# Delta-rule attention slots on one Trainium2 core: two groups of transposes and one copy change places

## The chip, the core and the metric

The kernel runs on one core of a Trainium2 chip. The core has five engines, each with an in-order instruction queue: Tensor (matrix products and transposes into PSUM; the profile calls it PE, and its weight loads PEld), Vector (DVE), Scalar (ACT), GpSimd (POOL) and Sync (SP), which here only issues DMAs. The engines wait for each other through semaphores. The metric is the time on the device in microseconds (us), lower is better. The granted clock of Tensor is given as a share of its full speed, 2.4 GHz.

## What is computed

The reference is a two-layer model on an input of 4 x 512 tokens of width 256. Each layer adds an attention and a feed-forward branch to its input:

```python
x  = L0_attn_x                                # 4 x 512 x 256
xn = _layernorm(x)
x  = x + _L0_attn_ref(xn, ...) + _L0_ffn_ref(xn, ...)
xn = _layernorm(x)
x  = x + _L1_attn_ref(xn, ...) + _L1_ffn_ref(xn, ...)

# attention, in both layers: 16 key heads, 32 value heads of 128
mixed = silu(causal_conv_of_4_taps(xn @ W_qkv))     # -> q, k, v
q = l2norm(q) * 128 ** -0.5;  k = l2norm(k)
def step(S, (q, k, v, g, beta)):                    # one token
    S = S * exp(g)
    u = (v - k @ S) * beta
    S = S + outer(k, u)
    return S, q @ S
# then a root-mean-square norm, a gate silu(z) and @ W_out
```

The change touches the attention only. The feed-forward branches are a mixture of six experts (layer 0) and a table-coded network (layer 1).

## The kernel before

**Tiling.** The recurrence over tokens is replaced by its chunked form. A sequence is cut into 4 chunks of 128 tokens (`CHUNKS`), the four sequences are worked on side by side (`BATCH`), and each key head (`KHEADS`, 16) serves a group of two value heads (`GROUPS`). One pass of the function `body` over (key head h, chunk c) is a slot; a layer has 64 of them, in the order of `steps`, and the file has one `body` for each engine, whose statements are that engine's queue. Within a slot an engine does the attention of slot (h, c) and, mixed into it, the preparation of the next one, (nh, ncn): the projections of q, v and z, the convolution, the transposes of keys and queries, their squares for the norms, and the decays.

**A slot on Tensor** (all in `body` of `block.tensor`). `fill(t)` is a projection of six matrix products (L837), t = 0 to 4. Between the five of them lie the steps of the inverse of a 128 x 128 triangular matrix, which is put together from its blocks: L896 (first group, its result is copied by Scalar at L1098), L909 (second group, read by Vector at L1292), L921 and L926 (turned blocks and the third group, which wait for Vector's L1292), and L939 (the last corner, which waits for Scalar's copies of Z, L1103, and of X, L1115). The last term of projection 2 stands behind the wait for L1292. The next slot's keys are transposed by `keys_token_major` (L849, four transposes) ahead of L909, the queries by `queries_token_major` (L859) behind the wait for Z and ahead of L939. Then follow, in chunks 1 to 3, the products with the state (L950, which waits for the corner copies L1124, and L957), the key products L866, then L969, L977 (not in chunk 3), L981, the values' transposes L877 (which wait for Vector's L1259), the outputs' transposes L996 and the output projection L1005. In layer 1 the gate is taken first (`gate_first`): L996 waits for Vector's L1279. In layer 0 L996 waits for Scalar's L1168, and L1005 for L1279.

**A slot on Scalar.** Its queue is: scaled keys of group 0 (L1093), the first convolution input (`copy_mix`, L1030 and L1031), the copy of Z's first part (L1098), scaled keys of group 1, then `square_keys` (the copy L1068 of the transposed keys and four squares L1059), `copy_mix` of 1, the queries' silu (L1051), `copy_mix` of 2, `copy_right` (L1115), two `copy_z` (L1103), `copy_left` (L1119), in chunk 2 three weight splits (L1040), silu of z (L1045), `square_queries` (four squares, L1059), `copy_corner` (L1124), silu of z and of the values, and later the copies for the second half of the slot. In chunk 3 there are no scaled keys.

**A slot on Vector.** Convolution of q (three L1204, which start when Scalar's L1031 of that tile is done), L1292 on the second group's result, convolution of value head 0, `key_columns` (L1212 to L1218), convolution of value head 1, in chunk 2 weight splits (L1344), `query_columns` (L1224, which waits for the queries' squares), the diagonals (L1232), in chunks 1 to 3 L1309 on the product L950, the decay scans (L1243), L1252, L1255, L1259, the state's update (L1265 or L1271), the gates (L1279) and the residual (L1337).

**Order.** It is written out by hand in the three bodies. Sync loads rows, keys, products and inverse blocks for the next slots; GpSimd computes the scaled queries and two powers. Neither is touched by the change.

Of the kernel before, what the change touches and what calls it, by code (L numbers as in the profile page):

```python
# [623 lines left out]
def delta_attention(nc, m, L, d):  # L624

    gate_first = L == 1
    with ExitStack() as ctx:
# [103 lines left out]
        def pj_bank(c, t):  # L731

            return pj[:, (c + t) % 2, :]

        def following(h, c):
            return (h, c + 1) if c + 1 < CHUNKS else (h + 1, 0)

        with nc.Block() as block:
# [83 lines left out]
            def _(pe):  # L822
                def project(h, c, t, k, first, terms=(0, 1, 2)):


                    q = 4 * h + c
                    if k == 0 and terms[0] == 0:
                        if c == 0:
                            pe.wait_ge(w_high_ok, PROJS * h + t + 1)
                            pe.wait_ge(w_low_ok, PROJS * h + t + 1)  # L830
                        if t >= 2 or not first:
                            pe.wait_ge(pj_read, PROJS * q + t - 1)
                    at = slice(HALO + c * P, HALO + (c + 1) * P)
                    pairs = ((w_high, m.x_high), (w_high, m.x_low), (w_low, m.x_high))
                    for n in terms:
                        wt, xt = pairs[n]
                        ins = nc.tensor.matmul(pj_bank(c, t), wt[:, k, t, :], xt[:, k, :, at],  # L837
                                               start=(k == 0 and n == 0), stop=(k == KD - 1 and n == 2))
                    if k == KD - 1 and terms[-1] == 2:
                        ins.then_inc(proj_mm, 1)  # L840

                def keys_token_major(h, c, first):

                    q = 4 * h + c
                    pe.wait_ge(k_in[c % 2], 16 * (2 * h + c // 2 + 1))
                    if not first:
                        pe.wait_ge(vn_ok, 2 * q - 1)
                    for b in range(BATCH):
                        ins = nc.tensor.transpose(kk[:, 0, bank(b)], kq[:, c % 2, b, 0, :], eye)  # L849
                    ins.then_inc(ktok_mm, 1)  # L850

                def queries_token_major(h, c, first):

                    q = 4 * h + c
                    pe.wait_ge(q_silu, q + 1)
                    if not first:
                        pe.wait_ge(vn_ok, 2 * q)
                    for b in range(BATCH):
                        ins = nc.tensor.transpose(kk[:, 1, bank(b)], kq[:, c % 2, b, 1, :], eye)  # L859
                    ins.then_inc(qtok_mm, 1)  # L860
# [19 lines left out]
                def body(h, c, first, last):  # L880
                    it = 4 * h + c
                    nh, ncn = following(h, c)

                    def fill(t):
                        if not last:
                            project(nh, ncn, t, 0, False)
                            project(nh, ncn, t, 1, False)
# [11 lines left out]
                    fill(1)  # L899
                    pe.wait_ge(xd_in, 64 * (it + 1))  # L900
                    pe.wait_ge(z32_cp, it + 1)
                    if not last:
                        keys_token_major(nh, ncn, False)
                    if not first:
                        for g in range(GROUPS):
                            pe.wait_ge(res_ok[g], BATCH * it)
# [3 lines left out]
                                                   Z[half(g), 0, part(b)], start=True, stop=True)  # L910
                    ins.then_inc(dx_mm, 1)
                    if not last:
                        project(nh, ncn, 2, 0, False)
                        project(nh, ncn, 2, 1, False, (0, 1))
                    pe.wait_ge(w_blocks_in, 64 * (it + 1))
# [8 lines left out]
                    for b in range(BATCH):  # L924
                        for g in range(GROUPS):
                            ins = nc.tensor.matmul(gb[HALF:, 0, g, part(b)], corner_a[half(g), c % 2, b, :],  # L926
                                                   W[half(g), b, 0:HALF], start=True, stop=True)
                            if b == BATCH - 1:
                                ins.then_inc(z64_mm[g], 1)
                    fill(3)  # L930
                    pe.wait_ge(x_in, 32 * (it + 1))
                    pe.wait_ge(x_cp, 4 * it + 1)
                    for g in range(GROUPS):
                        pe.wait_ge(z_cp[g], it + 1)
                    if not last:
                        queries_token_major(nh, ncn, False)
                    for b in range(BATCH):
                        for g in range(GROUPS):
                            ins = nc.tensor.matmul(gb[half(g), 0, g, part(b)], Z[HALF:, g, part(b)],  # L939
# [80 lines left out]
            def _(act):  # L1020
# [21 lines left out]
                def silu_z(h, c, g):  # L1042
                    q = 4 * h + c
                    act.wait_ge(proj_mm, PROJS * q + CONVS + g + 1)
                    nc.scalar.activation(zT[:, c % 2, g, :], pj_bank(c, CONVS + g), ACT.Silu).then_inc(pj_read, 1)  # L1045
# [9 lines left out]
                def square(w):  # L1055

                    for b in range(BATCH):
                        n = w * BATCH + b
                        ins = nc.scalar.activation(sq_kq[:, bank(n)], kk[:, w, bank(b)], ACT.Square,  # L1059
                                                   accum_out=ss_kq[:, n:n + 1])  # L1060
                    return ins
# [9 lines left out]
                def square_queries(h, c):  # L1071
                    q = 4 * h + c
                    act.wait_ge(qtok_mm, q + 1)
                    square(1).then_inc(q_sq, 1)
# [21 lines left out]
                def copy_z32(it):  # L1096
                    act.wait_ge(z32_mm, it + 1)
                    nc.scalar.activation(Z[:, 0, 0:BATCH * HALF], gb[:, 1, 0, 0:BATCH * HALF],  # L1098
                                         ACT.Copy).then_inc(z32_cp, 1)
# [18 lines left out]
                def copy_left(it):  # L1118
                    nc.scalar.activation(corner(X, low, low), turned(1, low, HALF), ACT.Copy).then_inc(x_cp, 1)  # L1119

                def copy_corner(it):
                    for g in range(GROUPS):
                        act.wait_ge(x64_mm[g], it + 1)
                        nc.scalar.activation(by4(X[low, g, :])[:, :, high],  # L1124
                                             gb[half(g), 0, g, 0:BATCH * HALF].rearrange("p (b n) -> p b n", b=BATCH),
                                             ACT.Copy, scale=-1.0).then_inc(x_cp, 1)

                def body(h, c, first, last):
                    it = 4 * h + c
                    nh, ncn = following(h, c)  # L1130
                    if c < CHUNKS - 1:
                        scaled_keys(h, c, 0)
                    if not last:
                        copy_mix(nh, ncn, 0, False)
                    copy_z32(it)
                    if c < CHUNKS - 1:
                        scaled_keys(h, c, 1)
                    if not last:
                        square_keys(nh, ncn, False)
                        copy_mix(nh, ncn, 1, False)  # L1140
                        silu_conv(nh, ncn, 0)
                        copy_mix(nh, ncn, 2, False)
                    copy_right(it)
                    for g in range(GROUPS):
                        copy_z(g, it)
                    copy_left(it)
                    if c == 2 and h < KHEADS - 1:
                        for t in range(CONVS):
                            split_weights(h + 1, t)
                    if not last:  # L1150
                        silu_z(nh, ncn, 0)
                        square_queries(nh, ncn)
                    copy_corner(it)
                    if not last:
                        silu_z(nh, ncn, 1)
                        for t in range(1, CONVS):
                            silu_conv(nh, ncn, t)
                    if c == 2 and h < KHEADS - 1:
                        for t in range(CONVS, PROJS):
                            split_weights(h + 1, t)  # L1160
                    for g in range(GROUPS):
                        act.wait_ge(y_mm[g], it + 1)
                        nc.scalar.activation(y[:, g, :], gb[:, 0, g, :], ACT.Copy,  # L1163
                                             scale=-1.0 if c else 1.0).then_inc(y_cp[g], 1)
                    if not gate_first:
                        for g in range(GROUPS):
                            act.wait_ge(o_mm[g], it + 1)
                            nc.scalar.activation(oT[:, g, :], gb[:, 1, g, :], ACT.Copy).then_inc(o_cp[g], 1)  # L1168
                    for g in range(GROUPS):
                        act.wait_ge(sso_mm[g], it + 1)  # L1170
                        for b in range(BATCH):
                            ins = nc.scalar.activation(Z[:, g, bank(b)], gb[:, 0, g, bank(b)], ACT.Square,  # L1172
                                                       accum_out=ss_o[:, g, b:b + 1])
                        ins.then_inc(o_sq[g], 1)
                    if not last:
                        scaled_values(nh, ncn)
# [639 lines left out]
```

## Time and profile before

| | us |
|---|---|
| median of 3 runs | 4951.69 (4949.87 to 4952.98) |
| the profiled execution's own time | 4951.72 |
| its span, first to last instruction | 4949.9 |
| Tensor busy | 4443.0 (90%) |
| Vector busy | 3852.1 (78%) |
| Scalar busy | 2999.4 (61%) |
| GpSimd busy | 692.1 (14%) |

The profiled execution agrees with the median, so times read in its trace can be set against either. The first slot of layer 0 begins at about 782 us and the last of layer 1 at about 4917 us; between the layers lie the feed-forward branches, the norm and the preparation of the inverse blocks. Slots of the same chunk look alike through a layer, so a slot can be read once for each chunk.

How to read a trace row: start in us from the start of the span, duration, engine, line of the kernel, operation, the tile written and the tiles read, their shapes, and how many instructions are merged in the row. Brackets give the idle time of the engine just before, and the instruction that ended it by its semaphore; "issue" is an idle time for which the profile names none. Tensor's instructions are pipelined, and their ends are modelled.

### The profile page before, as it was taken

To read this page: it belongs to the slowest core of one execution; us is meant where nothing else is said; L and a number is where in the kernel's file an instruction comes from. 1 tells how busy PE (TensorE), PEld (TensorE's weight loads), DVE (VectorE), ACT (ScalarE), POOL (GpSimd) and SP (SyncE) were. 2 spreads that over 40 slices of the span, in tenths; PEclk is the share of its full clock that TensorE was granted. 3 is DMA by queue.
4 is the path that set the end of the run, shared out by engine and by line. 5 is a ranking of instruction groups with operands and counts; after the bars stand their busy time and mean duration, and the time that the engine had idled before them with its cause. 6 is when DMAs were issued, how large, how long until landed. Compare 5 with 4: busy or idle time off the path is not lost. (4 is left out here: it accounts for less than half of the span.)

```text
span 4949.9 us, 93402 instructions
## 1 busy us (share of the span) xinstructions
PE 4443.0 (90%) x32596; PEld 3643.5 (74%) x32596; DVE 3852.1 (78%) x8126; ACT 2999.4 (61%) x9834; POOL 692.1 (14%) x740
## 2 busy tenths in 40 slices
PE   5899937999999999999969988299999999999998
PEld 3577736888888888888845877188888888887887
DVE  6838887888888888888841587788888888888886
ACT  1145526777777777777611555366666676767665
POOL 0000001122121221212200000021212122221211
PEclk8999968999999999999969999599999999999999
DMA  1035543222232222222200555322222222222222
GB/s 56 28 96 158 166 123 92 77 82 75 79 87 72 80 71 85 80 77 80 61 30 15 144 165 166 100 77 77 83 73 79 72 81 74 80 76 80 71 80 63
DMA packets 637757, 422.56 MB, mean 85 GB/s; under 512 B 458344, under 2 KB 533656, under 8 KB 636846
## 3 DMA queue, kind: packets, MB, share of 16 engines
q1 hardware_dynamic: 637294, 416.62, 29.2%
q8 instruction: 262, 4.29, 0.4%
q14 instruction: 201, 1.65, 0.1%
HBM read 296.24 MB, written 120.16 MB: 84 GB/s over the span
## 5 line engine op out<-in xcount | busy, mean ns | idle before, releaser
L1204 DVE SCALAR_TENSOR_TENSOR conv_l<-mix_l,taps_l,conv_l 128x512 f32<-128x512 f32 x1152 | 865.0, 751 | 270.3 <-ACT conv_l L1031 243.0
L837 PE MATMUL pj_l<-x_high,w_high_l 128*128 128x512 f32 x1280 | 588.2, 460 | 160.3 <-ACT w_high_l L1040 160.3
L837 PE MATMUL pj_l<-x_high,w_low_l 128*128 128x512 f32 x1280 | 521.1, 407 | 41.8 <-DVE W_l L1292 41.8
L837 PE MATMUL pj_l<-x_low,w_high_l 128*128 128x512 f32 x1280 | 512.5, 400 | 0.0
L1406 POOL TENSOR_TENSOR fac_l<-den_l,powers 128x4 f32<-128x4 f32 x256 | 258.0, 1008 | 1783.7 <-DVE den_l L1327 1779.8
L1005 PE MATMUL gb_l<-wo_l,gT_l 128*128 128x256 f32 x2048 | 478.7, 384 | 0.0
L1172 ACT ACTIVATE Z_l<-gb_l 128x128 f32<-128x128 f32 x1024 | 267.9, 289 | 307.1 <-PE gb_l L996 307.1
L1005 PEld LDWEIGHTS gb_l<-wo_l,gT_l 128*128 128x128 f32 x2048 | 372.6, 190 | 67.8 <-ACT Z_l L1172 24.4
L1337 DVE SCALAR_TENSOR_TENSOR x<-gb_l,fac_l,x 128x256 f32<-128x256 f32 x1024 | 413.0, 477 | 9.0
L837 PEld LDWEIGHTS pj_l<-x_high,w_high_l 128*128 128x128 f32 x1280 | 241.6, 189 | 231.3 <-ACT w_high_l L1040 160.9
L1163 ACT ACTIVATE y_l<-gb_l 128x512 f32<-128x512 f32 x256 | 153.2, 598 | 397.8 <-PE gb_l L969 393.1
L837 PEld LDWEIGHTS pj_l<-x_high,w_low_l 128*128 128x128 f32 x1280 | 241.6, 189 | 148.4 <-issue 93.3
L1243 DVE TENSOR_TENSOR_SCAN decay_l<-rows_l,diag_b_l 128x512 f32<-128x512 f32 x256 | 300.3, 1215 | 0.0
L1082 ACT ACTIVATE vn_l<-kk_l,ncol_l 128x128 f32<-128x128 f32 x1024 | 284.7, 438 | 17.2 <-PE kk_l L877 17.2
L1030 ACT ACTIVATE mix_l<-pj_l 128x512 f32<-128x512 f32 x384 | 238.8, 622 | 69.3 <-PE pj_l L837 58.9
L1031 ACT ACTIVATE conv_l<-pj_l,taps_l 128x512 f32<-128x512 f32 x384 | 274.6, 715 | 0.0
L1379 POOL TENSOR_TENSOR ncol_l<-n_l,powers 128x4 f32<-128x4 f32 x128 | 130.3, 1018 | 1013.2 <-DVE n_l L1212 1013.2
L837 PEld LDWEIGHTS pj_l<-x_low,w_high_l 128*128 128x128 f32 x1280 | 242.9, 190 | 35.2
L1059 ACT ACTIVATE diag_b_l<-kk_l 128x128 f32<-128x128 f32 x1024 | 268.0, 280 | 0.1
L981 PE MATMUL gb_l<-ap_l,y_l 128*128 128x128 f32 x2048 | 267.2, 276 | 0.0
L620 DVE TENSOR_TENSOR lane_t_l<-lane_t_l,lane_step_l 128x336 f32<-128x336 f32 (+16 forms) x540 | 252.1, 467 | 18.6
L617 DVE TENSOR_TENSOR lane_step_l<-lane_k_l,lane_t_l 128x336 f32<-128x336 f32 (+16 forms) x540 | 251.2, 465 | 18.6
(203 smaller groups left out, 10449.0 us busy)
## 6 DMA issues: line engine op xcount, KB each, us to landing
rows_l<-rows_dram SPq DMA_DIRECT2D x128, 1024.0 KB, 5.5
k_dram<-kT_l SPq DMA_DIRECT2D x128, 256.0 KB, 2.3
kk_dram<-key_kkS_l SPq DMA_DIRECT2D x128, 256.0 KB, 2.4
kq_l<-k_dram SPq DMA_DIRECT2D x128, 256.0 KB, 3.2
kkS_l<-kk_dram SPq DMA_DIRECT2D x128, 256.0 KB, 5.7
w_raw_l<-in_wx SPq DMA_DIRECT2D x32, 640.0 KB
own_dram<-key_kkS_l SPq DMA_DIRECT2D x1024, 16.0 KB, 1.7
lane_k_l<-own_dram SPq DMA_DIRECT2D x32, 512.0 KB, 4.4
```

Of the source, the lines that this page charges most:

```text
L620: nc.vector.tensor_tensor(t[:, :, j + 1:, 0:j], t[:, :, j + 1:, 0:j], prod, ALU.subtract).then_inc(solve, 1)
L837: ins = nc.tensor.matmul(pj_bank(c, t), wt[:, k, t, :], xt[:, k, :, at], start=(k == 0 and n == 0), stop=(k == KD - 1 and n == 2))
L981: ins = nc.tensor.matmul(gb[:, 1, g, bank(b)], y[:, g, bank(b)], ap[:, c % 2, g, b, 1, :], start=(c == 0), stop=True, skip_group_check=True)
L1005: ins = nc.tensor.matmul(gb[:, b // 2, g, (b % 2) * DIM:(b % 2 + 1) * DIM], gT[:, g, bank(b)], wo[:, g, :], start=True, stop=True)
L1031: nc.scalar.activation(conv[:, t, :], pj_bank(c, t), ACT.Copy, scale=taps[:, h, t, HALO:HALO + 1]).then_inc(pj_read, 1)
L1059: ins = nc.scalar.activation(sq_kq[:, bank(n)], kk[:, w, bank(b)], ACT.Square, accum_out=ss_kq[:, n:n + 1])
L1082: ins = nc.scalar.activation(vn[:, g, bank(b)], kk[:, g, bank(b)], ACT.Copy, scale=ncol[:, b:b + 1])
L1172: ins = nc.scalar.activation(Z[:, g, bank(b)], gb[:, 0, g, bank(b)], ACT.Square, accum_out=ss_o[:, g, b:b + 1])
L1204: ins = nc.vector.scalar_tensor_tensor(out, mix[:, t, :, i:i + P], wt(i), out, ALU.mult, ALU.add)
L1243: nc.vector.tensor_tensor_scan(decay[:, g, :], rows[:, c % 2, g, 0, :], diag_b[:, g, :], 0.0, ALU.mult, ALU.add).then_inc(decay_ok, 1)
L1337: nc.vector.scalar_tensor_tensor(xt, gb[:, b // 2, g, (b % 2) * DIM:(b % 2 + 1) * DIM], fac[:, g, b:b + 1], xt, ALU.mult, ALU.add).then_in ...
L1406: nc.gpsimd.tensor_tensor(fac[:, g, :], den[:, g, :], m.powers[:, 1, :], ALU.pow).then_inc(fac_ok[g], 1)
```

## The change

Three pieces of the hand-written order change; no instruction is added, removed or altered. On Tensor, `keys_token_major` of the next slot stands behind L909 instead of ahead of it, and `queries_token_major` stands ahead of the waits for the X and Z copies instead of behind them; the waits inside these two functions move with them. On Scalar, `copy_corner` stands ahead of `square_queries` in chunks 1 to 3, and stays behind it in chunk 0.

```diff
@@ -899,8 +899,6 @@
                     fill(1)
                     pe.wait_ge(xd_in, 64 * (it + 1))
                     pe.wait_ge(z32_cp, it + 1)
-                    if not last:
-                        keys_token_major(nh, ncn, False)
                     if not first:
                         for g in range(GROUPS):
                             pe.wait_ge(res_ok[g], BATCH * it)
@@ -910,6 +908,7 @@
                                                    Z[half(g), 0, part(b)], start=True, stop=True)
                     ins.then_inc(dx_mm, 1)
                     if not last:
+                        keys_token_major(nh, ncn, False)
                         project(nh, ncn, 2, 0, False)
                         project(nh, ncn, 2, 1, False, (0, 1))
                     pe.wait_ge(w_blocks_in, 64 * (it + 1))
@@ -928,12 +927,12 @@
                             if b == BATCH - 1:
                                 ins.then_inc(z64_mm[g], 1)
                     fill(3)
+                    if not last:
+                        queries_token_major(nh, ncn, False)
                     pe.wait_ge(x_in, 32 * (it + 1))
                     pe.wait_ge(x_cp, 4 * it + 1)
                     for g in range(GROUPS):
                         pe.wait_ge(z_cp[g], it + 1)
-                    if not last:
-                        queries_token_major(nh, ncn, False)
                     for b in range(BATCH):
                         for g in range(GROUPS):
                             ins = nc.tensor.matmul(gb[half(g), 0, g, part(b)], Z[HALF:, g, part(b)],
@@ -1149,8 +1148,12 @@
                             split_weights(h + 1, t)
                     if not last:
                         silu_z(nh, ncn, 0)
+                    if c > 0:
+                        copy_corner(it)
+                    if not last:
                         square_queries(nh, ncn)
-                    copy_corner(it)
+                    if c == 0:
+                        copy_corner(it)
                     if not last:
                         silu_z(nh, ncn, 1)
                         for t in range(1, CONVS):
```

## Rows read from the trace of the kernel before

**Rows 1.** Busy time by stage, layer 1: stretch, length, engines, granted clock, DMA.

```profile
3300.00:4900.00 1600.00, 1534.84 (x12831) 1295.36 (x12831) 1325.70 (x2981) 1100.11 (x4020) 317.68 (x339) 1.00 0.27 77
```

**Rows 2.** Timeline of Scalar, layer 1, chunk 1; the last row from chunk 2.

```profile
4103.53 0.60 ACT L1068 ACTIVATE ktok_l<-kk_l 128x512 f32<-128x512 f32 x1
...
4108.12 0.63 ACT L1103 ACTIVATE Z_l<-gb_l 64x256 f32<-64x256 f32 x2
...
4109.78 0.28 ACT L1059 ACTIVATE diag_b_l<-kk_l 128x128 f32<-128x128 f32 x1
...
4110.70 0.22 ACT L1059 ACTIVATION_READ_ACCUMULATOR diag_b_l<-kk_l 128x1 f32 x1
4110.80 0.79 ACT L1124 ACTIVATE X_l<-gb_l 64x256 f32<-64x256 f32 x2
...
4138.78 0.26 ACT L1059 ACTIVATE diag_b_l<-kk_l 128x128 f32<-128x128 f32 x1
```

**Rows 3.** Timeline of Tensor, layer 1, chunk 1, first part of the slot.

```profile
4102.86 0.60 PE L849 MATMUL kk_l<-eye,kq_l 128*128 128x128 f32 x4
4103.39 0.68 PE L909 MATMUL gb_l<-Z_l,Xd_l 64*64 64x64 f32 x16
...
4105.78 0.47 PE L837 MATMUL pj_l<-x_high,w_low_l 128*128 128x512 f32 x1 [0.33 <-DVE W_l L1292]
...
4108.47 0.39 PE L837 MATMUL pj_l<-x_high,w_low_l 128*128 128x512 f32 x1
4109.11 0.63 PE L859 MATMUL kk_l<-eye,kq_l 128*128 128x128 f32 x4 [0.26 <-issue]
4109.67 0.68 PE L939 MATMUL gb_l<-X_l,Z_l 64*64 64x64 f32 x16
```

**Rows 4.** Timeline of Vector, layer 1, chunk 1; the last two rows from chunk 2.

```profile
4102.03 2.33 DVE L1204 SCALAR_TENSOR_TENSOR conv_l<-mix_l,taps_l,conv_l 128x512 f32<-128x512 f32 x3 [1.51 <-ACT conv_l L1031]
4104.39 1.24 DVE L1292 TENSOR_SCALAR W_l<-gb_l 32x128 f32<-32x128 f32 x4
4106.26 2.33 DVE L1204 SCALAR_TENSOR_TENSOR conv_l<-mix_l,taps_l,conv_l 128x512 f32<-128x512 f32 x3 [0.63 <-ACT conv_l L1031]
...
4111.23 0.16 DVE L1224 TENSOR_SCALAR qcol_l<-ss_kq_l 128x4 f32<-128x4 f32 x1
...
4112.90 2.16 DVE L1309 SCALAR_TENSOR_TENSOR vn_l<-gb_l,run_columns_l,vn_l 128x128 f32<-128x128 f32 x8 [0.30 <-PE gb_l L950]
...
4140.34 0.17 DVE L1224 TENSOR_SCALAR qcol_l<-ss_kq_l 128x4 f32<-128x4 f32 x1
...
4141.82 0.87 DVE L1309 SCALAR_TENSOR_TENSOR vn_l<-gb_l,run_columns_l,vn_l 128x128 f32<-128x128 f32 x3
```

**Rows 5.** Timeline of Tensor at the ends of four slots, layer 1, chunks 0 to 3.

```profile
4095.26 0.66 PE L996 MATMUL gb_l<-eye,gT_l 128*128 128x128 f32 x4 [0.46 <-DVE gT_l L1279]
...
4123.37 0.66 PE L996 MATMUL gb_l<-eye,gT_l 128*128 128x128 f32 x4 [0.20 <-DVE gT_l L1279]
...
4152.96 0.65 PE L996 MATMUL gb_l<-eye,gT_l 128*128 128x128 f32 x4 [0.88 <-DVE gT_l L1279]
...
4177.76 0.86 PEld L877 LDWEIGHTS kk_l<-eye,vT_l 128*128 128x128 f32 x8 [0.23 <-DVE ap_l L1259]
```

**Rows 6.** Timeline of Vector's gates and Tensor's output projections, layer 0, chunks 0 to 2.

```profile
1658.16 1.28 DVE L1279 TENSOR_TENSOR gT_l<-zT_l,gb_l 128x512 f32<-128x512 f32 x2
1659.31 3.82 PE L1005 MATMUL gb_l<-wo_l,gT_l 128*128 128x256 f32 x16
...
1685.79 1.28 DVE L1279 TENSOR_TENSOR gT_l<-zT_l,gb_l 128x512 f32<-128x512 f32 x2
1687.19 3.82 PE L1005 MATMUL gb_l<-wo_l,gT_l 128*128 128x256 f32 x16
...
1715.15 1.28 DVE L1279 TENSOR_TENSOR gT_l<-zT_l,gb_l 128x512 f32<-128x512 f32 x2
1715.89 3.81 PE L1005 MATMUL gb_l<-wo_l,gT_l 128*128 128x256 f32 x16
```

## What the change will do to the time

> **What bounds the kernel now.** I read four views. First the table of stages: over 1600 us of the second layer's attention Tensor is busy 1535 us, Vector 1326, Scalar 1100, at a granted clock of 1.00 [rows 1]. By shares this is Tensor's stage. Then, because the change only reorders work inside a slot, I read one slot in order of time on each engine, and looked for where an engine stands still and who ends it. A slot is one of the 64 steps (key head, chunk) of a layer; I write its times as the trace has them, for chunk 1 of one head.
>
> Scalar [rows 2]: from the copy of the transposed keys (L1068, 4103.53) to the end of the corner copies (L1124, 4111.59) it runs without one idle mark. It is an in-order queue: keys' copy and squares, the convolution inputs, the copies of Z, silu, queries' squares, corner. The keys' transposes end on Tensor at 4102.86 + 0.60 = 4103.46 [rows 3], and the keys' copy starts 0.07 later. So that whole stretch of eight us hangs on the keys' transposes, in chunk 1.
>
> Vector [rows 4]: the second convolution starts at 4106.26 after 0.63 idle, ended by Scalar's L1031, in that stretch. From there to L1224 at 4111.23 nothing stops it; then comes 0.30 idle before L1309, ended by Tensor's L950, and after that it is loaded to the end of the slot. In chunk 2 the same place has no idle mark.
>
> The end of the slot [rows 5]: in layer 1 the second half of Tensor's L996 waits for Vector's gate L1279: 0.46 us in chunk 0, 0.20 in chunk 1, 0.88 in chunk 2. In chunk 3 it is L877 at 4177.76 whose weights load waits 0.23 for Vector's L1259. So in all four slots of a layer 1 head Tensor ends its slot behind Vector, and Vector behind Scalar, and Scalar behind the keys' transposes. The holes Tensor has earlier in the slot are not what sets the period. In layer 0, L1005 waits for the first gate: the gate pair starts at 1658.16, 1685.79 and 1715.15, one gate takes about 0.68 (half of a pair's 1.28 and an overlap of 0.08), so it is ready at 1658.84, 1686.47 and 1715.83; L1005 starts at 1659.31, 1687.19 and 1715.89 [rows 6]. With 0.06 for the handover, Vector is 0.41, 0.66 and 0 us ahead in chunks 0, 1 and 2.
>
> **The change, part by part.** No instruction is added or removed, no DMA is moved; waits travel with their groups.
>
> *Keys' transposes behind L909.* Before, they take Tensor at 4102.86 and L909 follows at 4103.39. After, L909 stands first. It lasts 0.68 with some 0.07 of overlap, so the transposes start about 0.61 later and, since a group of 64-wide tiles does not start as tightly behind a projection as they do, up to 0.69 later; lower bound 0.60, I take s = 0.65, the middle. Who gains: L909's reader on Vector is L1292, which starts at 4104.39, right behind the convolution that began at 4102.03 and lasts 2.33 [rows 4]: end 4104.36. An earlier L909 (it ended at 4104.07) gives at most 0.03. So the hole of 0.33 before the last projection term, ended by L1292 [rows 3], stays: Tensor has the same work ahead of that wait in either order. Who loses: Scalar. Queued behind the keys' copy are both convolution inputs, the Z copies and silu, and Vector's second convolution waits for one of them. All move by s: Z's second copy ends at 4108.12 + 0.63 + 0.65 = 4109.40.
>
> *Queries' transposes ahead of the wait for Z.* They now start at 4109.11, and the projection before them would have let them start at 4108.71 (its terms follow each other every 0.24, the last from 4108.47). This 0.40 us hole, put down to issue, is filled. L939 then has to wait for Z's copies itself. The transposes start 0.36 after the copies' end (4109.11 against 4108.12 + 0.63 = 4108.75) [rows 2, 3], with six conditions to pass; L939 will have four, so I give it 0.27 to 0.36: it starts at 4109.67 to 4109.76. It starts at 4109.67 today. The gain of this edit, 0.40, is eaten by s exactly. It costs nothing: the queries' silu stands ahead of the Z copies in Scalar's queue, so it is done when they are needed at 4108.71.
>
> *Corner ahead of squares, chunks 1 to 3.* The squares start at 4109.78 today, right behind the silu [rows 2]. The corner takes their place: 4109.78 + 0.65 = 4110.43. The corner copies run from 4110.43 to 4111.22 (L939 ends at 4109.67 + 0.68 = 4110.35, in time); the squares start 0.75 behind their start, the overlap taken off, and last 1.14 (4109.78 to 4110.70 + 0.22), to 4112.32. Today they end at 4110.92 and Vector takes L1224 at 4111.23, not waiting. After the change Vector would be there at 4111.88 and stands until 4112.36, 0.04 being the handover. L1224 to L1309 takes 1.48 in chunk 2 where no idle is marked [rows 4], of which 0.12 is a gap that I can't assign, so 1.36 to 1.48: L1309 starts at 4113.72 to 4113.84, not 4112.90. That is 0.82 to 0.94 later; I take 0.88. What the earlier corner buys is L950, and Tensor waits for Vector at L996 anyway. In chunk 2 both queues hold weight splits ahead of this place: the squares start at 4138.78 today, so they will end at 4138.78 + 0.65 + 0.75 + 1.14 = 4141.32, and L1224 comes at 4141.36 instead of 4140.34, 1.02 later; no idle behind it takes any of that. Chunk 3 is like chunk 1. Chunk 0 keeps its order: Vector moves by 0.65, and has no L1309 whose idle could absorb any.
>
> **The sum.** Layer 1: each slot's end moves with Vector: 0.65 + 0.88 + 1.02 + 0.88 = 3.43 us a head. Layer 0: chunk 0 has 0.41 of lead, so 0.24; chunk 1 0.88 - 0.66 = 0.22; chunk 2 1.02; chunk 3 0.88, since I take its tie at L877 to be that of layer 1: 2.36. Sixteen heads: 54.9 + 37.8 = 92.7. The last slot of each layer has no next one (1.8 less) and the last head's chunk 2 has no weight split, as chunk 1 (0.9 less): 90 us. The profiled execution took 4951.72 us (span 4949.9), the median of the runs is 4951.69, so both give 5042 us, 1.8% slower. With the low ends (s 0.60, 1.36) the same sum gives 79 us, with the high ends (0.69, 1.48) 99 us: 5031 to 5050.
>
> The Trainium skill, page "Perfetto Trace Analysis", section "Identifying the Most-Contended Engine", says to take the engine with the highest occupancy as the bottleneck, though it warns that matmul busy time misleads for Tensor. By that, closing Tensor's holes gains, which is rival A; the waits at L996 and L877 disagree with it here.
>
> **Rivals.**
> A. *Tensor is the bound* and the filled holes count; ends faster. The place is L859: 0.40 us in 126 slots, 50 us. For: Tensor is busy 96% [rows 1]. Against: Z's copies are Scalar's, and Scalar follows the keys' transposes. It decides from an s under about 0.05. As layer 1 waits at L996 all the same, only layer 0's 63 slots can bring it: 25 us, 4927 us; in both layers 50 us, 4902 us.
> B. *Only the keys' delay counts*: the squares come in time though they stand behind the corner (Scalar catching up by 0.5 us). Then L1309 in chunks 1 and 3 moves by 4111.88 + 1.42 - 4112.90 = 0.40, chunks 0 and 2 by 0.65: 2.10 a head in layer 1, and 0.24 + 0 + 0.65 + 0.40 = 1.29 in layer 0: 54 us less 1, 5005 us. For: Scalar is busy only 1100 of 1600 us [rows 1]. Against: its idle time does not lie between the keys' copy and the corner.
> C. *Nothing moves*: the filled hole and the delay cancel at L939, as worked out, and the way over Vector has slack that I don't see. Then 4952 us. For: layer 0's leads in chunks 0 and 1. Against: the marks at L996 and the tie at L877.
> D. *The clock falls too.* The granted clock is 1.00 over the stage though chunk 2 has a hole of 0.88 [rows 1, 5]; this hole would grow to 1.9 us. If Tensor came out of each on the lower level (1.2 GHz), L1005's pass of 3.82 us [rows 6] would take up to twice that in 32 slots: 122 us more, 5164 us.
> "TensorE: Matmul & The Clock Gate" of the Trainium skill, section "What's actually happening", says that idling throttles the array's clock; no run here shows it for holes of this size.
>
> **How the numbers follow.** The likeliest is the sum as worked out, chance 0.65: 5042. B has 0.14, times between the two included; A 0.10; C 0.06; D 0.05. The range goes from just under B to above the sum's high end: 5003 to 5058; it leaves out A, C and D, 0.21, about 2 in 10. A measurement of this kernel can tell some 0.2% (10 us) from no change. Faster by more: 0.10. Within: 0.06. Slower by more: 0.84.
>
> **What would show it.** In the changed profile: keys' copy on Scalar 0.60 to 0.69 later in the slot, with an idle mark ended by the transposes in every chunk; no issue hole at the queries' transposes, and a new one before L939, which starts at the same time in the slot as today; Vector's idle before the second convolution 1.2 to 1.3 instead of 0.63; a new idle of about 0.5 before L1224, ended by Scalar's squares, in chunks 1 to 3; L996's holes in layer 1 near 1.1, 1.1 and 1.9. The sum is wrong if L1292 starts earlier with L909, if Scalar's stretch shows idle marks that swallow s, or if L996 and L877 no longer wait for Vector.

## The result and the profile after

The changed kernel takes 5044.42 us (median of 4, 5042.76 to 5048.51) against 4951.65 us before: the ratio is 1.0187, with a 95% interval of 1.0172 to 1.0202. It is slower by 1.9%; the profiled execution took 5042.76 us, with a span of 5041.0. All engines execute the same numbers of instructions. The profile's table of busy times, with the share of the span in parentheses:

```profile
PE 4451.6 (88%) x32596; PEld 3647.0 (72%) x32596; DVE 3855.5 (76%) x8126; ACT 2992.0 (59%) x9834; POOL 691.6 (14%) x740
```

The busy table of the stretch of [rows 1] after the change has the granted clock still at 1.00, and Tensor at 1490 of 1600 us instead of 1535:

```profile
3300.00:4900.00 1600.00, 1490.03 (x12384) 1252.58 (x12384) 1286.49 (x2895) 1058.94 (x3876) 307.55 (x328) 1.00 0.26 74
```

The slot of chunk 1 that answers to [rows 2 to 4] starts at 4164.27 (its L896; before, 4100.72). Most line numbers are shifted: L907 is the old L909, L938 the old L939, L949 the old L950, L995 the old L996, L1067 the old L1068, L1102 the old L1103, L1123 the old L1124, L1207 the old L1204, L1227 the old L1224, L1312 the old L1309, L1262 the old L1259, L1282 the old L1279. Timeline of Tensor:

```profile
4164.27 0.69 PE L896 MATMUL gb_l<-Te_l,ap_l 128*64 128x64 f32 x16
...
4166.49 0.68 PE L907 MATMUL gb_l<-Z_l,Xd_l 64*64 64x64 f32 x16
4167.11 0.66 PE L849 MATMUL kk_l<-eye,kq_l 128*128 128x128 f32 x4
4169.34 0.47 PE L837 MATMUL pj_l<-x_high,w_low_l 128*128 128x512 f32 x1 [0.39 <-DVE W_l L1295]
...
4172.26 0.60 PE L859 MATMUL kk_l<-eye,kq_l 128*128 128x128 f32 x4
4173.16 0.68 PE L938 MATMUL gb_l<-X_l,Z_l 64*64 64x64 f32 x16 [0.30 <-ACT Z_l L1102]
```

Timeline of Scalar, same slot:

```profile
4167.80 0.60 ACT L1067 ACTIVATE ktok_l<-kk_l 128x512 f32<-128x512 f32 x1 [0.81 <-PE kk_l L849]
...
4172.39 0.63 ACT L1102 ACTIVATE Z_l<-gb_l 64x256 f32<-64x256 f32 x2
...
4174.02 0.78 ACT L1123 ACTIVATE X_l<-gb_l 64x256 f32<-64x256 f32 x2
4174.82 0.28 ACT L1058 ACTIVATE diag_b_l<-kk_l 128x128 f32<-128x128 f32 x1
...
4175.75 0.22 ACT L1058 ACTIVATION_READ_ACCUMULATOR diag_b_l<-kk_l 128x1 f32 x1
```

Timeline of Vector, same slot:

```profile
4167.95 1.24 DVE L1295 TENSOR_SCALAR W_l<-gb_l 32x128 f32<-32x128 f32 x4
4170.53 2.33 DVE L1207 SCALAR_TENSOR_TENSOR conv_l<-mix_l,taps_l,conv_l 128x512 f32<-128x512 f32 x3 [1.34 <-ACT conv_l L1030]
...
4176.00 0.17 DVE L1227 TENSOR_SCALAR qcol_l<-ss_kq_l 128x4 f32<-128x4 f32 x1 [0.41 <-ACT diag_b_l L1058]
4177.40 0.87 DVE L1312 SCALAR_TENSOR_TENSOR vn_l<-gb_l,run_columns_l,vn_l 128x128 f32<-128x128 f32 x3
```

The times below are differences to the slot's start. The keys' copy on Scalar stood at 4103.53 - 4100.72 = 2.81 and stands at 3.53, behind 0.81 of idle ended by the keys' transposes. The second convolution on Vector stood at 5.54 and stands at 6.26; its idle time grew from 0.63 to 1.34. Tensor's L938 stood at 8.95 and stands at 8.89: the queries' transposes have filled the hole ahead of it (L859 has no bracket now), and a wait for Z (0.30) has taken its place. L1227 stood at 10.51 and stands at 11.73, and L1312 stood at 12.18 and stands at 13.13.

The ends of slots that answer to [rows 5], layer 1, chunks 0 to 3 (timeline of Tensor; the last row is a weights load):

```profile
4158.82 0.66 PE L995 MATMUL gb_l<-eye,gT_l 128*128 128x128 f32 x4 [0.54 <-DVE gT_l L1282]
...
4187.87 0.66 PE L995 MATMUL gb_l<-eye,gT_l 128*128 128x128 f32 x4 [0.97 <-DVE gT_l L1282]
...
4215.25 1.09 PE L877 MATMUL kk_l<-eye,vT_l 128*128 128x128 f32 x8 [0.29 <-DVE ap_l L1262]
4216.88 0.66 PE L995 MATMUL gb_l<-eye,gT_l 128*128 128x128 f32 x4 [0.53 <-DVE gT_l L1282]
4218.51 0.66 PE L995 MATMUL gb_l<-eye,gT_l 128*128 128x128 f32 x4 [0.97 <-DVE gT_l L1282]
...
4244.31 0.86 PEld L877 LDWEIGHTS kk_l<-eye,vT_l 128*128 128x128 f32 x8 [1.25 <-DVE ap_l L1262]
```

In chunk 3 the wait for Vector went from 0.23 to 1.25; in chunk 2 Tensor now waits three times (0.29, 0.53 and 0.97, where it was 0.88 once). The first and the last instruction of L896 give the totals over the 64 slots of a layer: layer 0 went from 782.4 to 2470.2 before and from 782.1 to 2506.7 after, 36.8 us more; layer 1 from 3204.7 to 4917.8 before and from 3238.3 to 5008.9 after, 57.5 us more. That is 94.3 us; the span grew by 91.1 us, so the program outside the attention slots took 3.2 us less.

By the distance from one slot's L896 to the next (the median of each chunk), the slots of chunks 0 to 3 became longer by 0.73, 0.95, 1.04 and 0.99 us in layer 1, and by 0.31, 0.18, 0.97 and 0.98 in layer 0.

### The profile page after: what moved, and what is told of

Read it like the earlier page. It is cut to its first block and busy times, and to the rows that moved or that the text cites. A ratio compares the mean times of both kernels' runs of the same rounds, so it can differ in the third digit from the quotient of the medians.

```text
span 5041.0 us, 93402 instructions
## 1 busy us (share of the span) xinstructions
PE 4451.6 (88%) x32596; PEld 3647.0 (72%) x32596; DVE 3855.5 (76%) x8126; ACT 2992.0 (59%) x9834; POOL 691.6 (14%) x740
## 5 line engine op out<-in xcount | busy, mean ns | idle before, releaser
L1207 DVE SCALAR_TENSOR_TENSOR conv_l<-mix_l,taps_l,conv_l 128x512 f32<-128x512 f32 x1152 | 864.9, 751 | 378.5 <-ACT conv_l L1030 351.2
```

What stands on the lines that cost most here:

```text
L1207: ins = nc.vector.scalar_tensor_tensor(out, mix[:, t, :, i:i + P], wt(i), out, ALU.mult, ALU.add)
```

## The experiments

Each kernel is told by its difference to the kernel before, and each ratio is to runs of that kernel on the same chip. A slot's length is again the distance from its L896 to the next one. Theory T: a slot ends behind Vector, Vector runs behind Scalar, Scalar behind the keys' transposes; Tensor's early holes are free. Rival A: Tensor's own holes set the period. Rival B: only the keys' delay counts, the corner's place costs nothing.

### The three parts one by one

**e1_keys_only**

```diff
-                    if not last:
-                        keys_token_major(nh, ncn, False)
...
                     ins.then_inc(dx_mm, 1)
                     if not last:
+                        keys_token_major(nh, ncn, False)
```

> Only the keys' transposes move behind L909; queries and corner stay as before. Theory T (the slot ends behind Vector, Vector behind Scalar, Scalar behind the keys' transposes): the keys' copy on Scalar comes 0.71 us later in the slot, as measured in the changed kernel, the Z copies with it, and since the queries' transposes and L939 still wait behind them, Tensor is late by the same 0.7. So no lead of layer 0 absorbs anything: 0.7 us in each of 126 slots, 89 us, 5040 us, as slow as the whole change. Rival A (Tensor's own holes set the period): the work ahead of each wait of Tensor is the same, so 4952 us. Rival B (only the keys' delay counts in the whole change): 5044 us, and then the corner alone costs nothing.

Measured: 5045.47 us, ratio 1.0177 (1.0162 to 1.0193) to the runs of the kernel before on the same chip, 4955.29 us. That is +88 us of that base, where T expected 89 and A nothing. The slots of each chunk and layer are longer by 0.70 to 0.74 us. Timeline of Tensor in this kernel, layer 1: the second half of the outputs' transposes (L995) in chunk 2, and the queries' transposes in chunk 3:

```profile
4115.23 0.66 PE L995 MATMUL gb_l<-eye,gT_l 128*128 128x128 f32 x4 [0.87 <-DVE gT_l L1278]
...
4129.81 0.63 PE L859 MATMUL kk_l<-eye,kq_l 128*128 128x128 f32 x4 [0.98 <-ACT Z_l L1102]
4130.36 0.68 PE L938 MATMUL gb_l<-X_l,Z_l 64*64 64x64 f32 x16
```

The hole that was 0.26 by the mark in chunk 1 [rows 3] is 0.98 here: the Z copies come 0.72 later and everything on Tensor behind them too. Rival A, by which the time stays, is out. This one part, alone, costs as much as the whole change. By which way the delay reaches the slot's end this run doesn't tell: Tensor is late by the Z copies and Vector by its second convolution, by the same amount, and the mark at L995 is what it was (0.87; before, 0.88). The changed kernel does tell it, since there L938 is in time and the slot ends late all the same.

**e2_queries_only**

```diff
                     fill(3)
+                    if not last:
+                        queries_token_major(nh, ncn, False)
                     pe.wait_ge(x_in, 32 * (it + 1))
                     pe.wait_ge(x_cp, 4 * it + 1)
                     for g in range(GROUPS):
                         pe.wait_ge(z_cp[g], it + 1)
-                    if not last:
-                        queries_token_major(nh, ncn, False)
```

> Only the queries' transposes move ahead of the wait for Z; keys and corner stay as before. Theory T: L939 comes 0.37 us earlier in the slot (8.59 instead of 8.96 after L896). In layer 0, chunks 0 and 1 gain 0.37 each, chunk 3 about 0.3 by way of L950 and L1309, chunk 2 nothing; in layer 1 chunks 1 and 3 gain the 0.30 of idle that Vector has before L1309, chunks 0 and 2 nothing, since they end behind Vector. Sum 1.04 + 0.60 = 1.6 us a head, 26 us: 4926 us (4915 to 4935). Rival A: 0.40 us in all 126 slots: 4902 us.

Measured: 4934.73 us, ratio 0.9964 (0.9951 to 0.9978), 18 us faster by the ratio, where T expected 26 (in its range of 17 to 37) and A 50. Timeline of Tensor, chunk 2, layer 1:

```profile
4121.79 0.60 PE L859 MATMUL kk_l<-eye,kq_l 128*128 128x128 f32 x4
4122.32 0.68 PE L939 MATMUL gb_l<-X_l,Z_l 64*64 64x64 f32 x16
...
4125.58 1.16 PE L950 MATMUL gb_l<-S_l,kq_l 128*128 128x128 f32 x8 [0.97 <-ACT X_l L1124]
```

L939 does follow at once. In chunk 2 the time it gained is lost again at L950, which waits 0.97 for the corner copies, where in the kernel before it waited 0.54:

```profile
4140.62 2.05 PE L950 MATMUL gb_l<-S_l,kq_l 128*128 128x128 f32 x16 [0.54 <-ACT X_l L1124]
```

In chunks 1 and 3 too L950 starts only when the corner is copied, and Vector's L1309 keeps 0.19 of its 0.30 idle:

```profile
4097.87 2.16 DVE L1309 SCALAR_TENSOR_TENSOR vn_l<-gb_l,run_columns_l,vn_l 128x128 f32<-128x128 f32 x8 [0.19 <-PE gb_l L950]
```

So those slots gain 0.12 or 0.13 instead of the 0.30 that was expected (0.37 in layer 0's chunk 1); the shortfall of 8 us is there. In layer 0's chunk 0, where Tensor does not wait for Vector at the end, the filled hole is worth 0.42.

**e3_corner_only**

```diff
                         silu_z(nh, ncn, 0)
-                        square_queries(nh, ncn)
-                    copy_corner(it)
+                    if c > 0:
+                        copy_corner(it)
+                    if not last:
+                        square_queries(nh, ncn)
+                    if c == 0:
+                        copy_corner(it)
```

> Only the corner copies move ahead of the squares in chunks 1 to 3. Theory T: in chunks 1 and 3 Scalar stands 0.6 us for L939, then the squares end 1.1 us later than before and L1309 starts 0.8 us later; in chunk 2 0.3 us later. Layer 1 loses 0.83 + 0.31 + 0.85, layer 0 0.17 + 0.31 + 0.8 after its lead: 3.3 us a head, 50 us, 5002 us (4992 to 5012). Rival A: nothing, or a gain of up to 17 us by the wait of L950 in chunk 2: 4935 to 4952 us. Rival B: 4952 us.

Measured: 5000.51 us, ratio 1.0100 (1.0085 to 1.0116), +49.6 us, where T expected 50, and A and B nothing or a gain. Timelines of Scalar and Vector, chunk 1 (L1228 is the old L1224):

```profile
4140.78 0.78 ACT L1124 ACTIVATE X_l<-gb_l 64x256 f32<-64x256 f32 x2 [0.53 <-PE gb_l L939]
4141.58 0.28 ACT L1059 ACTIVATE diag_b_l<-kk_l 128x128 f32<-128x128 f32 x1
```

```profile
4142.76 0.17 DVE L1228 TENSOR_SCALAR qcol_l<-ss_kq_l 128x4 f32<-128x4 f32 x1 [1.04 <-ACT diag_b_l L1059]
```

Scalar stands 0.53 for L939 with the squares queued behind the corner, and Vector, which had no wait at this place, stands 1.04 for the squares.

**e4_keys_queries** is the whole change without the corner's part.

```diff
 # the changed kernel, with this undone:
-                    if c > 0:
-                        copy_corner(it)
-                    if not last:
                         square_queries(nh, ncn)
-                    if c == 0:
-                        copy_corner(it)
+                    copy_corner(it)
```

> The whole change without its corner part. Theory T: keys' copy 0.71 us later, L939 where it was. Vector reaches L1224 without a wait, so L1309 starts 0.46 to 0.5 later in chunks 1 and 3 instead of 0.95; in chunk 2 the corner stands behind the squares, L950 comes 0.75 later than before and L1309 0.7. Layer 1 loses 0.73 + 0.46 + 0.72 + 0.50, layer 0 0.31 + 0 + 0.65 + 0.45: 3.8 us a head, 58 us, 5010 us (5000 to 5020). Rival B: as the whole change, 5044 us. Rival A: below 4952 us.

Measured: 5023.41 us, ratio 1.0140 (1.0125 to 1.0156), +69 us, above T's range (48 to 68; 58 expected) and below what B expected (93). Timelines of Tensor and Vector, chunk 1 (L1308 is the old L1309):

```profile
4163.79 2.05 PE L949 MATMUL gb_l<-S_l,kq_l 128*128 128x128 f32 x16 [0.40 <-ACT X_l L1123]
```

```profile
4164.99 1.13 DVE L1308 SCALAR_TENSOR_TENSOR vn_l<-gb_l,run_columns_l,vn_l 128x128 f32<-128x128 f32 x4 [0.19 <-PE gb_l L949]
```

I had missed that with a late Scalar the corner, behind the squares, holds L949 in chunks 1 and 3 as well. Layer 0's chunk 1, for which nothing was expected, became 0.60 longer. So the corner's new place does something for the change it came with: it removes this 0.40, and puts a wait of 0.41 before L1227 in its stead. With it layer 0's chunk 1 is 0.42 shorter, and all other slots of chunks 1 to 3 are longer, by 0.24 to 0.35. In sum it costs 1.0187 - 1.0140, 0.5% or 23 us (19 by the spans of the two profiles). Rival B, by which it costs nothing, is out, and T stands with a smaller price for this part than its cost alone.

### The queue on Scalar

If the keys' delay costs because of what is queued behind the keys' copy, then it must cost nothing once the first thing behind it is put in front. That is one swap of two statements; the work is the same.

**e5_full_mix_first** is the changed kernel with it.

```diff
                     if not last:
-                        square_keys(nh, ncn, False)
                         copy_mix(nh, ncn, 1, False)
+                        square_keys(nh, ncn, False)
                         silu_conv(nh, ncn, 0)
```

> The whole change, and on Scalar the keys' copy and squares stand behind the second convolution input instead of ahead of it (the work is the same, only that order differs). Theory T: the delay of the keys' transposes costs because the second convolution input stands behind the keys' copy. With the input ahead, Scalar does 1.1 us of other work while the transposes run, is at the Z copies when it was before the change, and Vector's second convolution starts right behind L1292, at 4.95 after L896 instead of 6.26. What is left is the corner ahead of the squares, which lets L1224 start at about 11.15. Layer 1: -0.3, +0.4, +0.3, +0.4; layer 0: -0.4, -0.3, +0.3, +0.35 against the kernel before: 0.75 us a head, 12 us, 4963 us (4950 to 4975). Rival E (the later keys' transposes cost in themselves, on Tensor or by the norms of the keys): stays near 5044 us.

Measured: 4951.25 us, ratio 1.0001 (0.9991 to 1.0010) to the kernel before, where T expected 4963 (4950 to 4975) and rival E, by which late transposes cost in themselves, 5044: the swap gives back the whole 1.9%, and E is out. That the ratio is 1 is a balance and no return to the old slots: by length, chunk 0 is shorter than before the change by 0.46 us in layer 0 and 0.55 in layer 1, and chunk 3 is longer by 0.46. Timelines of Scalar and Vector, chunk 1:

```profile
4100.29 0.60 ACT L1029 ACTIVATE mix_l<-pj_l 128x512 f32<-128x512 f32 x1
4100.77 0.70 ACT L1030 ACTIVATE conv_l<-pj_l,taps_l 128x512 f32<-128x512 f32 x1
4101.34 0.61 ACT L1067 ACTIVATE ktok_l<-kk_l 128x512 f32<-128x512 f32 x1
```

```profile
4101.36 1.24 DVE L1295 TENSOR_SCALAR W_l<-gb_l 32x128 f32<-32x128 f32 x4
4102.64 2.33 DVE L1207 SCALAR_TENSOR_TENSOR conv_l<-mix_l,taps_l,conv_l 128x512 f32<-128x512 f32 x3
...
4108.90 0.17 DVE L1227 TENSOR_SCALAR qcol_l<-ss_kq_l 128x4 f32<-128x4 f32 x1 [1.20 <-ACT diag_b_l L1058]
```

The keys' copy has no bracket: the transposes are done when Scalar comes. Vector's second convolution has none either, where it had 0.63 even before the change, so the swap gives more than the keys' delay took at this place. What is left of the change is the corner, now a wait of 1.20 before L1227.

**e7_queries_mix_first** is e2_queries_only with the same swap.

```diff
                     if not last:
-                        square_keys(nh, ncn, False)
                         copy_mix(nh, ncn, 1, False)
+                        square_keys(nh, ncn, False)
```

> Queries' transposes ahead of the wait for Z, keys' transposes in their old place, corner behind squares as before, and on Scalar the second convolution input ahead of the keys' copy. Theory T: Vector's second convolution starts 0.6 us earlier, but L1224 then waits for the queries' squares (10.25 after L896, 0.3 earlier than before), and L1309 is held by L950, which waits for the corner behind the squares (10.87). So only chunk 0 of layer 1 gains beyond the run with the queries alone: 0.3 us in 16 slots, 5 us: 4929 us on a base of 4955 (ratio 0.995). Rival F (the start of the second convolution sets the slot's end in every chunk): 0.6 in 126 slots more, ratio 0.981.

Measured: 4904.61 us, ratio 0.9902 (0.9885 to 0.9919) on a base of 4952.12, 49 us faster; T expected 25 and F 94. F is out; T forecast half of the gain. I had kept Scalar's later times as they were. But before the keys' copy Scalar also stood a moment: its code there waits for the end of its own scaled keys and for the transposes, which end within 0.03 of each other in chunk 1, so the trace doesn't tell which of them held it. The convolution input has neither wait and starts 2.60 into the slot, where the keys' copy started at 2.81, and squares and corner come 0.22 earlier. The corner copies in e2_queries_only, whose slot starts at 4085.81, and in this kernel, slot from 4066.96 (timelines of Scalar, chunk 1): 10.03 and 9.81 into the slot.

```profile
4095.84 0.79 ACT L1124 ACTIVATE X_l<-gb_l 64x256 f32<-64x256 f32 x2
...
4076.77 0.78 ACT L1124 ACTIVATE X_l<-gb_l 64x256 f32<-64x256 f32 x2
```

L950 is free of the corner, and L1224 of the squares (timeline of Vector, chunk 1):

```profile
4076.91 0.17 DVE L1224 TENSOR_SCALAR qcol_l<-ss_kq_l 128x4 f32<-128x4 f32 x1
...
4078.80 1.39 DVE L1309 SCALAR_TENSOR_TENSOR vn_l<-gb_l,run_columns_l,vn_l 128x128 f32<-128x128 f32 x5 [0.52 <-PE gb_l L950]
```

**e9_late_z** is e7_queries_mix_first with this:

```diff
                     if not last:
-                        silu_z(nh, ncn, 0)
                         square_queries(nh, ncn)
                     copy_corner(it)
                     if not last:
+                        silu_z(nh, ncn, 0)
                         silu_z(nh, ncn, 1)
```

> As the run before it, and on Scalar the silu of z, group 0, stands behind squares and corner. Theory T: squares and corner are the end of Scalar's loaded stretch; 0.5 us less ahead of them lets L950 start at about 10.64 and L1224 at 9.9 to 10.0, both earlier than before by 0.45 to 0.6. Layer 1 gains 0.6, 0.45, 0.5, 0.45, layer 0 0.37, 0.37, 0.4, 0.45: 3.6 us a head, 57 us: ratio 0.9885 (0.986 to 0.992), the fastest of all. Rival A (Tensor's holes): as the queries alone, 0.996.

Measured: 4887.45 us, ratio 0.9867 (0.9851 to 0.9884), 66 us faster than the kernel before, where T expected 57 (0.986 to 0.992) and A 0.996.

**e10_late_z_keys_behind** is e9_late_z with the keys' transposes behind L909, as in e1_keys_only.

> The same kernel as e9_late_z with the keys' transposes behind L909, the part that cost 88 us alone. Theory T: Scalar reaches the keys' copy only at about 3.75 after L896, and the transposes end at 3.50, so the move costs nothing here: the ratio of e9_late_z within 0.2%. Rival E: some 80 us above it.

Measured: 4885.67 us, ratio 0.9869 (0.9853 to 0.9886). The move that cost 1.8% alone changes the ratio by 0.0002 here, far inside the interval. This is the cleanest of the tests: the edit is that of e1_keys_only, and what differs is only the order in Scalar's queue and the place of the queries' transposes. Timelines of Scalar and of Tensor, chunk 1, slot from 4048.46:

```profile
4052.11 0.61 ACT L1067 ACTIVATE ktok_l<-kk_l 128x512 f32<-128x512 f32 x1
...
4057.09 0.28 ACT L1058 ACTIVATE diag_b_l<-kk_l 128x128 f32<-128x128 f32 x1 [0.20 <-PE kk_l L859]
...
4058.10 0.78 ACT L1123 ACTIVATE X_l<-gb_l 64x256 f32<-64x256 f32 x2
```

```profile
4056.45 0.60 PE L859 MATMUL kk_l<-eye,kq_l 128*128 128x128 f32 x4
4056.98 0.68 PE L938 MATMUL gb_l<-X_l,Z_l 64*64 64x64 f32 x16
```

The keys' copy starts 3.65 into the slot, behind other work and after the transposes, and has no bracket. At the queries' transposes Scalar now waits for Tensor (0.20) and no longer the other way round: L938 has no bracket. e9_late_z and e10_late_z_keys_behind beat the kernel before by 1.3% and the changed one by 3.1%, with the same instructions.

## Why the prediction was right

5042 us were forecast, 5044.42 measured; by layer, 36 and 54 us after the last slots' deduction against 36.8 and 57.5. The mechanism held: the keys' delay goes through Scalar's queue to Vector and to the slot's end, and e10_late_z_keys_behind shows that it costs nothing once that way is closed. The number is a little closer than its terms: by chunk, 0.65, 0.88, 1.02 and 0.88 were forecast in layer 1 and 0.73, 0.95, 1.04 and 0.99 measured; in layer 0, 0.24, 0.22, 1.02 and 0.88, and 0.31, 0.18, 0.97 and 0.98 measured. The attention grew by 94.3 us, and the 3.2 us that went the other way elsewhere were not forecast: that part is luck. Point by point:

- *Who sets the slot's end.* Right: e1_keys_only and e3_corner_only cost 88 and 50 us though they leave Tensor's work as it was, and in the changed kernel the slot is late though L938 is not.
- *The keys' delay, s.* Forecast 0.65 (0.60 to 0.69), measured 3.53 - 2.81 = 0.72, just over the high end. Two sizes in it were off: L907 starts 2.22 after L896, where the transposes had started 2.14 after it, which only the high end had in it; and the transposes last 0.66 instead of 0.60 behind L907, which not even that had. It is the main term that was too small, and it runs through the chunks of layer 1: L1227 came 1.22 later in chunk 1 (1.13 forecast) and L1312 0.95 (0.88). The sum did not fall short by as much, because layer 0 gave the forecast's number and 3 us went elsewhere.
- *L1292 gains nothing from an earlier L909.* Right: L1295 starts 3.68 after L896, before 3.67.
- *L939 stays where it is.* Right, to 0.06, but by two sizes that were off against each other: the Z copies end 8.75 into the slot where 8.68 was forecast, and L938 follows their end after 0.14 where 0.27 to 0.36 was forecast. The change's gain at the queries' transposes, 0.40 a slot, was real (in e2_queries_only, without the keys' move, L939 starts 0.44 earlier, of which 18 us reach the time), and it was eaten by the keys' move.
- *Corner ahead of squares.* Right for the whole change, as a wait of 0.41 before L1227 against 0.48 forecast. That the earlier corner buys nothing was wrong: e4_keys_queries shows that without it L949 waits 0.40 and layer 0's chunk 1 is 0.42 longer. The forecast didn't need it, since it set the whole change against the kernel before, where the corner was in time.
- *L996's holes.* Forecast 1.1, 1.1 and 1.9. The delay did come, but split: in chunk 0 the mark is 0.54 with the first half of L995 late as well, in chunk 2 it is 0.29 + 0.53 + 0.97. One bracket alone would have misled.
- *Rivals.* A fell with e1_keys_only, B with e3_corner_only and e4_keys_queries, C with the result. D fell with the busy table: the granted clock is 1.00 with holes of 0.97 us. The single hole of 1.9 us that D was built on did not come (chunk 2's is in three parts), so no run here shows what the clock does behind such a hole. The Trainium skill's "Perfetto Trace Analysis", section "Identifying the Most-Contended Engine", picks the engine with the highest occupancy, but for Tensor it judges the headroom by the share of weight loads and not of matmuls. By matmuls Tensor led, with 1535 of 1600 us; by weight loads it has 1295, just under Vector's 1326 [rows 1]. The runs fit the second reading better: a move that leaves Tensor's work alone cost 88 us. The section "Identifying Dependency Chains" of the same page of the Trainium skill says to look at the semaphores that an instruction waits for; the brackets of the rows show that here, and they led to L996 and L877.

## What to carry to other kernels

When a step is moved behind another, look at the reader of the moved step and at all that is queued behind that reader; here 0.7 us of delay on a four-transpose step went through an in-order queue into a second engine and came out at the slot's end in every chunk (0.70 to 0.74 us in e1_keys_only). A hole on the busiest engine is worth something only if the engine doesn't wait for somebody else later in the same period, so look for the last wait of the period first. And if a delayed input can't be avoided, swap it in its reader's queue with work that is ready: that one swap was worth 1.9% in the changed kernel and 0.6% in e2_queries_only, where the input wasn't delayed.

## What the runs showed that I had not expected

A group of sixteen 64 x 64 products starts 2.22 us after L896 where a 128 x 128 transpose group started at 2.14, and the transposes behind it take 0.66 instead of 0.60: the two groups exchanged cost the second one's reader 0.72, not the 0.61 by which they follow each other. And a queue can lose time to waits that no bracket shows: before the change Scalar's keys' copy had none in chunk 1, yet taking it out of the place behind the scaled keys brought the end of that stretch forward by 0.22 us (e7_queries_mix_first against e2_queries_only).
